# The router of a mixture of experts as 16 more columns of the gate product, with tanh weights per tile

## What is computed

```
logits  = x @ gate_w.T                          # 1024 x 16
probs   = softmax(logits)
w, idx  = top_2(probs);  w = w / sum(w)
hidden  = silu(x @ g.T) * (x @ u.T)             # 1024 x 896, 56 per expert
out     = (hidden * w per expert) @ d.T         # 1024 x 512
```

## Time and profile before

| | |
|---|---|
| Median of 3 runs | 1212.45 us (1212.26 to 1212.47) |
| The profiled execution: its time | 1212.92 us |
| Its span in the profile | 1210.9 us |
| Granted TensorE clock, mean | 0.999 of full speed |
| Busy: TensorE, VectorE, ScalarE, GpSimd | 98%, 68%, 35%, 48% of the span |
| Expert stage | about 621 to 755 us of the span |

### The profile page before, as it was taken

The page is one execution under the profiler, slowest core; times in us unless marked ns, Lnnn a source line. Parts: engine busy times, 40 slices in busy tenths (PEclk is TensorE's granted clock), DMA queues, the critical chain, the costliest instruction groups (busy, mean ns, idle before and its releaser), DMA issues.

```text
span 1210.9 us, 16920 instructions
## 1 busy us (share of the span) xinstructions
PE 1190.4 (98%) x6210; PEld 948.8 (78%) x6210; DVE 823.8 (68%) x1434; ACT 427.3 (35%) x737; POOL 580.5 (48%) x400
## 2 busy tenths in 40 slices
PE   9999999999999999999999999999999999999998
PEld 7887878777777777777788888777777777777776
DVE  4656546898888888788973225676575767666795
ACT  5144142222213222222344113635444343445432
POOL 4522433766667576676254112335454545545500
PEclk9999999999999999999999999999999999999999
DMA  7844634712212221211211002122121212211201
GB/s 278 263 145 157 194 119 157 279 52 78 78 52 69 87 78 43 78 44 47 102 62 35 1 0 89 61 87 70 53 87 69 78 47 75 77 52 36 78 1 70
DMA packets 57457, 106.88 MB, mean 88 GB/s; under 512 B 3648, under 2 KB 36416, under 8 KB 52032
## 3 DMA queue, kind: packets, MB, share of 16 engines
q1 hardware_dynamic: 56880, 105.17, 25.3%
q0 software_dynamic: 384, 1.05, 0.2%
q10 hardware_dynamic: 144, 0.00, 0.0%
HBM read 78.95 MB, written 27.26 MB: 88 GB/s over the span
## 4 chain that ended last, share of the span: by engine, by line
PE 75%; DVE 10%; POOL 7%; issue 5%; ACT 2%; DMA 1%; SPq 0%; POOLq 0%; DVEq 0%; ACTq 0%
PE ps_b L226 11%; PE ps_b L228 11%; PE ps_b L227 11%; PE ps_q L226 11%; PE ps_q L228 10%; PE ps_q L227 10%; PE ps_s L934 4%; PE ps_b L961 3%; POOL qT L1246 2%; POOL wo_lo L1239 2%; PE ps_q L921 1%; POOL wq_lo L727 1%; POOL p_sb L779 1%; DVE o_lo L1410 1%; DVE x_sb L1419 1%
## 5 line engine op out<-in xcount | busy, mean ns | idle before, releaser
L226 PE MATMUL ps_q<-hT_hi,wq_hi 128*128 128x512 f32 x512 | 206.2, 403 | 0.0
L227 PE MATMUL ps_q<-hT_lo,wq_hi 128*128 128x512 f32 x512 | 199.8, 390 | 0.0
L228 PE MATMUL ps_q<-hT_hi,wq_lo 128*128 128x512 f32 x512 | 199.4, 389 | 0.0
L226 PE MATMUL ps_b<-wo_hi,o_hi 128*128 128x512 f32 x440 | 172.0, 391 | 3.4 <-POOL wo_lo L1239 3.4
L227 PE MATMUL ps_b<-wo_lo,o_hi 128*128 128x512 f32 x440 | 171.3, 389 | 0.0
L228 PE MATMUL ps_b<-wo_hi,o_lo 128*128 128x512 f32 x440 | 171.3, 389 | 0.0
L1246 POOL TENSOR_TENSOR qT<-q_t 128x512 f32<-128x512 f32 x64 | 89.9, 1405 | 75.8 <-DVE q_t L1345 70.5
L1410 DVE TENSOR_TENSOR o_lo<-ps_b,o_hi 128x512 fp32r<-128x512 f32 x128 | 82.1, 683 | 63.2 <-ACT o_hi L1135 62.0
L226 PEld LDWEIGHTS ps_q<-hT_hi,wq_hi 128*128 128x128 f32 x512 | 96.0, 188 | 33.2 <-issue 11.2
L1419 DVE SCALAR_TENSOR_TENSOR x_sb<-ps_b,gates,x_sb 128x512 f32<-128x512 f32 x120 | 86.1, 724 | 50.7 <-PE ps_b L228 50.2
L727 POOL TENSOR_TENSOR wq_lo<-wq_raw,wq_hi 128x512 fp32r<-128x512 f32 x64 | 90.2, 1415 | 54.2 <-ACT wq_hi L721 54.2
(11 more groups left out here) (300 smaller groups left out, 2481.8 us busy)
## 6 DMA issues: line engine op xcount, KB each, us to landing
wq_raw<-in_wq SPq DMA_DIRECT2D x16, 1024.0 KB, 4.8
wo_raw<-in_wo SPq DMA_DIRECT2D x16, 1024.0 KB, 4.8
kT<-kT_spill SPq DMA_DIRECT2D x32, 256.0 KB, 3.2
v_hi<-v_hi_spill SPq DMA_DIRECT2D x16, 512.0 KB, 3.7
v_lo<-v_lo_spill SPq DMA_DIRECT2D x16, 512.0 KB, 4.6
v_hi_spill<-vs_hi SPq DMA_DIRECT2D x12, 512.0 KB, 5.4
...
```

Source lines behind the costliest of these rows:

```text
L226: nc.tensor.matmul(dst, l_hi, r_hi, start=first, stop=False)
L227: nc.tensor.matmul(dst, l_hi, r_lo, start=False, stop=False)
L228: return nc.tensor.matmul(dst, l_lo, r_hi, start=False, stop=last)
```

## The change

The router's 16 rows are put ahead of the gate's 896, so that `up(i, r, 0)` makes 464 gate columns, of which the first 16 are the tile's logits. The router's own product, its load, its split, the turning of logits, softmax and Exp go. Instead, for each tile: ScalarE copies the 16 logits out of PSUM (`x_lg`); VectorE takes the 8 largest, minus the middle of the first two (`x_mid`), and a mask of 0.5 at the two largest (`x_at`); ScalarE takes tanh(logit - middle); VectorE makes (tanh + 1) x mask, which is the softmax over the two (`route`). The next tile's gate product waits until `x_lg` is read. The `Fori` loops are written out, tokens are read in `hT` directly and `tokens` is gone. TensorE's first `up` no longer waits for the last attention outputs to be added (only for those whose banks it writes), and the first `down` product stands behind tile 1's products instead of inside tile 2's. ScalarE's and GpSimd's splits of `down` change places; VectorE adds the last attention output ahead of two `hT_lo` instead of behind them; `down`'s load and the next layer's `wq` load wait for less. Some small tiles of layer 1 get other addresses.

```diff
+RG = NX + FI
...
-            f_hi, f_lo, sg, gu, hid = alloc(
-                a, ("f_hi", [P, 2, KC, P], FR), ("f_lo", [P, 2, KC, P], FR), ("sg", [P, 2, FH], F32), ("gu", [P, 2, FH], F32),
+            _, sg, gu, hid = alloc(
...
+            add_output(last, 1, 3)
             ln_low(dve, ln, 2)
             ln_low(dve, ln, 3)
-            add_output(last, 1, 3)
...
-            sp.wait_ge(*att[0]("q_done", J * 2 * G))
-            sp.dma_start(r_raw[:, :, :], router_t).then_inc(c["r_in"], 16)
             sp.wait_ge(*att[0]("y_done", 4 * (2 * G - 2)))
             sp.dma_start(u_raw[:, :, :], up_t).then_inc(c["u_in"], 16)
-            sp.wait_ge(c["w_hi"], 1 + 2 * FT)
-            sp.wait_ge(c["w_lo"], 1 + 2 * FT)
             sp.wait_ge(*att[0]("y_done", 4 * 2 * G))
             sp.dma_start(d_raw[:, :, :], down_t).then_inc(c["d_in"], 16)
             sp.wait_ge(c["w_hi"], len(splits))
             sp.wait_ge(c["w_lo"], len(splits))
-            sp.wait_ge(c["logits"], 2)
-            sp.wait_ge(c["hid"], 4)
             att_load_wq(sp, 1, 0)
...
-        splits = ([("r", 0)] + [(w, n) for w in "gu" for n in range(4)] + [(w, n) for w in "gu" for n in range(4, FT)]
+        splits = ([(w, n) for w in "gu" for n in range(4)] + [(w, n) for w in "gu" for n in range(4, FT)]
                   + [("d", n) for n in range(FT)])
-        GU_SPLITS = {("g", 0): 5, ("u", 0): 9, ("g", 1): 12, ("u", 1): 15}
-        SPLITS = {(0, -1): (0, 1, 2, 3, 4), (1, -1): (5, 6, 7, 8), (1, 0): (9, 10), (1, 1): (11, 12), (1, 2): (13,), (1, 3): (14,)}
+        GU_SPLITS = {("g", 0): 4, ("u", 0): 8, ("g", 1): 11, ("u", 1): 14}
+        SPLITS = {(0, -1): (0, 1, 2, 3), (1, -1): (4, 5, 6, 7), (1, 0): (8, 9), (1, 1): (10, 11), (1, 2): (12,), (1, 3): (13,)}
...
+                act.wait_ge(moe["w_lo"], 2 * FT)
...
-            def logits(h):
-
-                pe.wait_ge(*lns[1]("lo", (h + 1) * PAIRS))
-                for k in range(KC):
-                    last = three(ps_b[2][:, :], rT_hi[:, k, :], rT_lo[:, k, :], hT_hi[:, k, h * HALF:(h + 1) * HALF],
-                                 hT_lo[:, k, h * HALF:(h + 1) * HALF], k == 0, k == KC - 1)
-                last.then_inc(c["logits"], 1)
-
-            def logits_t():
-
-                pe.wait_ge(c["lgT"], 2)
-                for i in range(NT):
-                    last = nc.tensor.transpose(ps_h[0][:, i * NX:(i + 1) * NX], x_lgT[:, i * P:(i + 1) * P], ident[0:NX, 0:NX])
-                last.then_inc(c["lg_t"], 1)
-
             def up(i, r, half, between=None):
 
-                direct = isinstance(i, int) and i < 3
-                if half == 0 and not direct:
-                    pe.wait_ge(c["f_hi"], i - 2)
-                    pe.wait_ge(c["f_lo"], i - 2)
-                if not (isinstance(i, int) and i == 0):
+                if i > 0:
                     pe.wait_ge(c["gu"], 2 * i + half - 1)
+                if half == 0:
+                    pe.wait_ge(*lns[1]("lo", i + 1))
                 for bank, hi, lo, name in ((ps_q[half], gT_hi, gT_lo, "g_done"), (ps_b[half], uT_hi, uT_lo, "u_done")):
-                    if isinstance(i, int) and i == 0:
+                    if i == 0:
                         pe.wait_ge(c["w_lo"], GU_SPLITS[name[0], half])
+                        if name == "u_done":
+                            pe.wait_ge(*att[0]("y_added", (2 * G - 1) * PAIRS + half + 1))
+                    elif name == "g_done" and half == 0:
+                        pe.wait_ge(c["x_lg"], i)
+                    cols = slice(half * FH, (half + 1) * FH) if name == "u_done" else slice(half * (NX + FH), NX + (half + 1) * FH)
                     for k in range(KC):
-                        t_hi = hT_hi[:, k, i * P:(i + 1) * P] if direct else f_hi[:, r, k, :]
-                        t_lo = hT_lo[:, k, i * P:(i + 1) * P] if direct else f_lo[:, r, k, :]
-                        last = three(bank[:, 0:FH], t_hi, t_lo, hi[:, k, half * FH:(half + 1) * FH],
-                                     lo[:, k, half * FH:(half + 1) * FH], k == 0, k == KC - 1)
+                        tok = slice(i * P, (i + 1) * P)
+                        last = three(bank[:, 0:cols.stop - cols.start], hT_hi[:, k, tok], hT_lo[:, k, tok], hi[:, k, cols], lo[:, k, cols], k == 0, k == KC - 1)
                     last.then_inc(c[name], 1)
...
-            pe.wait_ge(*att[0]("y_added", 2 * G * PAIRS - 1))
-            pe.wait_ge(c["w_lo"], 1)
-            logits(0)
+            def turns(i):
+                ln_turn(pe, lns[1], i)
+                ln_turn(pe, lns[1], i + 1)
+
+            pe.wait_ge(*att[0]("y_added", (2 * G - 1) * PAIRS))
+            up(0, 0, 0)
+            turns(PAIRS)
+            up(0, 0, 1)
+            turns(PAIRS + 2)
+            up(1, 1, 0)
+            hidden_t(0)
+            up(1, 1, 1)
             pe.wait_ge(*att[0]("y_added", 2 * G * PAIRS))
-            up(0, 0, 0)
-            ln_turn(pe, lns[1], PAIRS)
-            ln_turn(pe, lns[1], PAIRS + 1)
-            up(0, 0, 1)
-            ln_turn(pe, lns[1], PAIRS + 2)
-            ln_turn(pe, lns[1], PAIRS + 3)
-            up(1, 1, 0)
-            logits(1)
-            up(1, 1, 1, logits_t)
-
-            up(2, 0, 0)
-            hidden_t(0)
-
-            def finish():
-                pe.wait_ge(c["w_lo"], len(splits))
-                down(0, 0)
-                hidden_t(1)
-
-            up(2, 0, 1, finish)
-            down(1, 1)
-            with pe.Fori(1, NT // 2 - 1) as m:
-                tile(2 * m + 1, 1)
-                tile(2 * m + 2, 0)
+            pe.wait_ge(c["w_lo"], len(splits))
+            down(0, 0)
+            for i in range(2, NT - 1):
+                tile(i, i % 2)
...
-            def logits(h):
-                act.wait_ge(c["logits"], h + 1)
-                nc.scalar.activation(x_lgT[:, h * HALF:(h + 1) * HALF], ps_b[2][0:NX, :], ACT.Copy).then_inc(c["lgT"], 1)
+            def logits(i, r):
+                act.wait_ge(c["g_done"], 2 * i + 1)
+                if i >= 2:
+                    act.wait_ge(c["x_rep"], i - 1)
+                nc.scalar.activation(x_lg[:, r, :], ps_q[0][:, 0:NX], ACT.Copy).then_inc(c["x_lg"], 1)
+
+            def tanh(i, r):
+                act.wait_ge(c["x_mid"], i + 1)
+                nc.scalar.activation(x_th[:, r, :], x_lg[:, r, :], ACT.Tanh, bias=x_mid[:, r:r + 1]).then_inc(c["x_th"], 1)
 
             def silu(i, half):
                 act.wait_ge(c["g_done"], 2 * i + half + 1)
                 if not (isinstance(i, int) and i == 0):
                     act.wait_ge(c["gu"], 2 * i + half - 1)
-                nc.scalar.activation(sg[:, half, :], ps_q[half][:, 0:FH], ACT.Silu, bias=zero_b[:, 0:1]).then_inc(c["silu"], 1)
-
-            def tokens(i, r):
-
-                if not (isinstance(i, int) and i == 3):
-                    act.wait_ge(c["u_done"], 2 * i - 2)
-                nc.scalar.activation(f_hi[:, r, :, :], hT_hi[:, :, bass.ts(i, P)].bitcast(F32), ACT.Copy).then_inc(c["f_hi"], 1)
+                own = slice(NX, NX + FH) if half == 0 else slice(0, FH)
+                nc.scalar.activation(sg[:, half, :], ps_q[half][:, own], ACT.Silu, bias=zero_b[:, 0:1]).then_inc(c["silu"], 1)
...
-                tokens(i + 1, 1 - r)
+                logits(i, r)
                 silu(i, 0)
+                tanh(i, r)
                 hidden_hi(i - 1)
                 silu(i, 1)
 
             ln_sd(act, lns[1], 1)
-            logits(0)
+            logits(0, 0)
             act.wait_ge(c["w_lo"], GU_SPLITS["g", 1])
             silu(0, 0)
+            tanh(0, 0)
             ln_high(act, lns[1], PAIRS)
             ln_high(act, lns[1], PAIRS + 1)
             silu(0, 1)
+            for m in (14, 15):
+                split_high(act, m)
             ln_high(act, lns[1], PAIRS + 2)
             ln_high(act, lns[1], PAIRS + 3)
-            for m in (15, 16):
+            for m in range(16, len(splits)):
                 split_high(act, m)
-            silu(1, 0)
-            for m in (17, 18, 19):
-                split_high(act, m)
-            logits(1)
-            silu(1, 1)
-            act.wait_ge(c["x_lg"], 1)
-            nc.scalar.activation(x_ex[:, :, :], x_lg[:, :, :], ACT.Exp, bias=zero_b[:, 0:1]).then_inc(c["x_ex"], 1)
-            for m in (20, 21):
-                split_high(act, m)
-            tokens(3, 1)
-            silu(2, 0)
-            hidden_hi(0)
-            silu(2, 1)
-            hidden_hi(1)
-            with act.Fori(1, NT // 2 - 1) as m:
-                tile(2 * m + 1, 1)
-                tile(2 * m + 2, 0)
+            for i in range(1, NT - 1):
+                tile(i, i % 2)
+            logits(NT - 1, 1)
             silu(NT - 1, 0)
+            tanh(NT - 1, 1)
             ln_sd(act, lns[2], 0)
...
+                if half == 0:
+                    pool.wait_ge(c["x_w"], i + 1)
...
+            for n in range(4):
+                split_low(pool, 2 * FT + n)
+            tile(0, 0)
+            for n in range(4, FT):
```

(53 more changed lines are left out.)

113 lines of the change are left out of this document (30 added, 83 removed).

## The result

| | before | changed |
|---|---|---|
| Median | 1212.5 us (1212.19 to 1214.74, 22 runs) | 1214.44 us (1213.57 to 1215.14, 22 runs) |
| Profiled execution: its time | 1212.92 us | 1215.09 us |
| Its span | 1210.9 us | 1213.3 us |

The ratio is 1.0014 with a 95% interval of 1.0008 to 1.0021: 0.08 to 0.21% slower. 1206.4 was forecast, 8.0 us less, and the time lies far outside the range.

What follows compares the result with a forecast made beforehand. TensorE, busy for 98% of the span, was taken as the bound. Gains of 7.8 us less 0.6, 0.9 and 0.7 gave -5.6, a replay -6.1; -6.0 off the 1212.45 median gave 1206.4 us, range 1204.6 to 1208.9.

Steps and rivals of the forecast that it cites:

- what costs nothing: Expert stage: VectorE's small operations, tanh, copies, splits, in-place `hT`, written-out loop and `down`'s load are hidden, adding 0 us.
- after the stage TensorE is the bound again: Layer 1, behind the expert stage: TensorE releases its loads, splits and norms, so all of it moves forward.
- The gains, 7.8: TensorE, expert stage: wait before first router product 1.0, router products 2.8 and 2.7, turning logits 0.6, first `hid` wait 0.7.
- new wait 1: Start of expert stage: TensorE waits 0.9 us for tile 0's `hid`, behind GpSimd's four `down` splits; bounds nothing to 2.2.
- 464 columns: Twelve gate matmuls in each of eight tiles get 16 more columns, 6 ns each: 0.6 us added; bounds nothing to 2.4.
- New wait 2: Last tile: route behind four statistics delays the root's table load and everything behind by 0.8, adding 0.7 us; bounds nothing to 1.3.
- The sum: Whole change: -7.8 + 0.6 + 0.9 + 0.7 = -5.6 us; a replay gave -6.1; -6.0 was taken.
- a wait of layer 1: Rival: layer 1's first scores wait for something TensorE does not release, giving the gain back; about 1212 us, chance 0.02.
- the load of `down`: Rival, expert stage: a late `down` load stops layer norm, `hid`, then TensorE; +7.5, 1213.9 us, chance 0.02.
- 0.96 for faster: Chance given to a whole-kernel time below 1210.0 us; within 0.2% got 0.03, slower 0.01.

Runs made afterwards that it cites:

- experiment 1: The changed kernel with its pad 52 bytes shorter, so everything behind stands at the addresses of the kernel before: 1205.77 us, ratio 0.9946.
- Experiment 6: On experiment 1: GpSimd weighs tile 0 behind two `down` splits, not four, 1205.51 us; then also VectorE's last-tile maximum and middle behind two statistics, not four, 1204.45 us.
- the repeated experiment 1: The same kernel as experiment 1, the changed one at the addresses of before, measured again later: 1205.62 us, ratio 0.9941.
- +128: The changed kernel with a longer pad, `wq` and all behind it 128 bytes higher than in the kernel before: 1212.99 us, ratio 1.0004.
- +32: The changed kernel with another pad length, `wq` and all behind it 32 bytes higher than in the kernel before: 1214.75 us, ratio 1.0017.
- -64: The changed kernel with a shorter pad, `wq` and all behind it 64 bytes lower than in the kernel before: 1210.07 us, ratio 0.998.

## Why the prediction was wrong

- **The step that failed** is one that isn't in the sum. The description of the change said that small tiles of layer 1 get other addresses; the part "what costs nothing" goes through the other edits and leaves this one out, and "after the stage TensorE is the bound again" took the attention's pace as given. The term that is missing is the address move, put at nothing without a reason. It costs 8.3 us in the queries' products, and 8.7 in the kernel. Against the medians: -6.6 for the change without the address move (experiment 1 against its runs of the kernel before, 1212.34), and 1214.44 - 1205.77 = +8.7 for the move.
- *The gains, 7.8.* Right in what goes away. The first gate product starts 0.22 us behind the last attention matmul with no wait; both router products, the turning of the logits and the wait for `hT_lo` ahead of the first are gone. The old wait for the first `hid` gives way to new wait 1.
- *464 columns.* Right. Twelve products take 628.10 - 625.58 = 2.52 us, 210 ns each, forecast 209. A tile takes 684.09 - 668.75 = 15.34, forecast 15.33 and the earlier trace rows 15.26 before. That this comes out to 0.01 is luck: the forecast kept the 203 ns of the other products, and at the addresses it assumed (experiment 1) a tile takes 15.45; the 64 bytes that slow the queries make `up`'s products faster. The Trainium skill (TensorE: Matmul & The Clock Gate, Back-to-back issue gap) gives 131 ns at 512 columns; no product of 512 columns in these traces comes near it: their mean steps lie between 227 and 233 ns.
- *New wait 1.* Right in mechanism, 0.72 for 0.9. Experiment 6 shows that the splits ahead of the first weighing make it.
- *New wait 2.* Right in mechanism, 0.68 for 0.9. On ScalarE the chain is the one replayed: tanh, the load of the root's table, the root, `hdT_hi`:

```profile
734.68 0.31 ACT L1778 ACTIVATE x_th<-x_lg,x_mid 128x16 f32<-128x16 f32 x1 [1.15 <-DVE x_mid L1873]
735.00 1.28 ACT L245 ACT_TABLE_LOAD   x1
736.30 0.30 ACT L245 ACTIVATE ln_sd<-ln_mv,eps_ln 128x4 f32<-128x4 f32 x1
736.50 0.96 ACT L1793 ACTIVATE hdT_hi<-ps_s 128x512 fp32r<-128x512 f32 x2
```

- *What costs nothing.* The small operations of VectorE, tanh, the loop written out and tokens read in place show no wait on TensorE in any tile. `down` arrived in time: its load was issued at 625.77 and took 7.3 us, and ScalarE's first split of it starts at 634.55. There is no table load at a tanh.
- *The sum.* -6.0 was forecast; the stage gives -6.3, and 129.03 - 134.72 = -5.7 in experiment 1, where a tile takes 15.45 instead of 15.34: the products of `up`, whose operands have also moved against each other, are there 204 ns apart instead of 201, and those of the gate 207 instead of 206. Two rivals have times near the result (1212 and 1213.9), but neither a wait of layer 1 nor the load of `down` took part. TensorE's longest waits behind the stage (from 756 us on) are the same in the changed kernel and before:

```profile
PE ps_q L919 <- ACT q_sq L1094: 0.7, 1, 0.7
...
PE ps_s L272 <- DVE ln_buf L264: 0.4, 1, 0.4
```

```profile
PE ps_q L921 <- ACT q_sq L1096: 0.7, 1, 0.7
...
PE ps_s L274 <- DVE ln_buf L266: 0.4, 1, 0.4
```

- *Chances.* 0.96 for faster held only if nothing outside the stage changes its pace, a condition with no chance of its own in the text.

The profiled executions differ in one more thing, at their very start. TensorE begins with 20 small transposes and a first group of 48 products. The changed kernel as made, then experiment 1:

```profile
1.56 4.53 PE L503 MATMUL ps_b<-ident 128*128 128x128 f32 x20 [1.56 <-POOL ident L327]
...
18.62 0.47 PE L224 MATMUL ps_q<-kw_hi,cT_hi 128*128 128x512 f32 x1 [0.82 <-DVE vs_lo L571]
```

```profile
1.56 3.78 PE L503 MATMUL ps_b<-ident 128*128 128x128 f32 x20 [1.56 <-POOL ident L327]
...
17.40 0.47 PE L224 MATMUL ps_q<-kw_hi,cT_hi 128*128 128x512 f32 x1 [0.83 <-DVE vs_lo L571]
```

As made, all 20 start 0.21 us apart; in experiment 1 the last six or so start 0.11 apart, though the granted clock of the profile reads 1.00 in both. Where the step halves differs even between two executions of one kernel: the repeated experiment 1 has it only at the last transpose, and its second row at 17.64. It doesn't follow the distance either: the slow +128 has that row at 17.41, +32 at 18.21, -64 at 18.61, and the kernel before at 18.82. So it is worth 1.2 us between the two profiles shown, and nothing here ties it to the change. From that row to the end of the span the kernel before takes 1192.07 us, the changed one 1194.65, and experiment 1 takes 1185.95: without the start the address move costs 8.7 and the rest of the change gains 6.1, where 6.0 was forecast. That these two agree so well is in part luck: a tile is 0.12 longer than forecast, the two waits are 0.4 shorter in sum, and 0.4 of the 6.1 lies outside the stage.
